# Preparing the state stage's weights on GpSimd instead of VectorE, at the start of the attention stage

## What is computed

```python
x = x + _L0_conv_ref(_gn(x), ...)   # 7x7 window attention, 4 heads of 8
x = x + _L1_conv_ref(_gn(x), ...)   # depthwise convolution, state-space scan, gated output
x = x + _L2_conv_ref(_gn(x), ...)   # triangular products over rows, layer norm, gate
x = x + _L3_conv_ref(_gn(x), ...)   # LSTM over the 28 rows
```

```python
def _L1_conv_ref(x, w1, dw, in_proj_w, conv1d_w, ..., x_proj_w, dt_proj_w, ..., out_proj_w, ..., w2, wout):
    x1 = _grouped_1x1(x, w1)                       # 4 groups of 8 channels
    x1 = depthwise_conv_3x3(x1, dw); x1 = silu(x1)
    x1 = _mamba(x1.reshape(B, H * W, D), ...)      # in_proj, 3-tap conv1d, x_proj, dt_proj, scan, out_proj
    x1 = layer_norm(x1) * gamma + beta
    return _grouped_1x1(x1 * silu(_grouped_1x1(x, w2)), wout)
```

## Time and profile before

| | |
|---|---|
| median of 3 runs | 478.54 us (476.59 to 478.87) |
| the profiled execution | 475.85 us, span 474.1 us |
| TensorE busy | 351.1 us, 74% |
| VectorE busy | 365.1 us, 77% |
| ScalarE busy | 299.8 us, 63% |
| GpSimd busy | 233.9 us, 49% |
| mean granted TensorE clock | 0.901 of full |
| attention stage | about 21 to 158 us |

### The profile page before, as it was taken

One profiled execution on the slowest core, in us unless ns is written; L12 is line 12 of the kernel. 1 busy time (PEld: TensorE's weight loads), 2 busy tenths in 40 slices (PEclk: granted clock), 3 DMA queues, 4 the chain that ended last, 5 costly groups with the idle time before them and its releaser, 6 DMA issues. The chain is left out here.

```text
span 474.1 us, 10021 instructions
## 1 busy us (share of the span) xinstructions
PE 351.1 (74%) x3480; PEld 230.4 (49%) x3480; DVE 365.1 (77%) x679; ACT 299.8 (63%) x583; POOL 233.9 (49%) x217
## 2 busy tenths in 40 slices
PE   5149888896789785985877647666795829888885
PEld 4037676675665332142233213222483519877774
DVE  3799999999797388799787999997576685544443
ACT  4327788887785899578758946347985253333432
POOL 4526868775673324966972999567081130000000
PEclk9997999998899999599897885768999668999999
DMA  6110000000223231022000000000030000111111
GB/s 147 5 18 3 3 1 0 0 1 0 59 60 70 51 87 29 1 60 58 1 0 1 0 1 0 0 0 1 3 68 3 1 0 11 20 19 22 22 19 24
DMA packets 24044, 10.29 MB, mean 22 GB/s; under 512 B 20576, under 2 KB 22368, under 8 KB 24016
## 3 DMA queue, kind: packets, MB, share of 16 engines
q1 hardware_dynamic: 23888, 9.93, 10.3%
q0 software_dynamic: 128, 0.01, 0.2%
HBM read 2.00 MB, written 1.61 MB: 8 GB/s over the span
## 5 line engine op out<-in xcount | busy, mean ns | idle before, releaser
L480 POOL TENSOR_TENSOR Pr<-Pr,rc 128x392 f32<-128x392 f32 x64 | 54.4, 883 | 32.2 <-DVE rc L1826 32.2
L511 POOL TENSOR_TENSOR YA<-YA,hC 128x784 f32<-128x784 f32 x27 | 51.7, 1914 | 32.4 <-DVE hC L1910 31.5
L1349 PE MATMUL pair<-BCf,sel 96*128 96x392 bf16 x128 | 38.4, 394 | 35.0 <-DVE Hs L1894 30.8
L1894 DVE TENSOR_TENSOR_SCAN Hs<-dA,pair 128x784 f32<-128x784 f32 x32 | 57.1, 1785 | 1.0
L1193 PE MATMUL pair<-ident,Pr 128*128 128x128 f32 x256 | 41.1, 293 | 13.2 <-ACT PT L715 9.0
L1349 PEld LDWEIGHTS pair<-BCf,sel 96*128 96x128 bf16 x128 | 10.2, 105 | 74.0 <-issue 71.6
L1193 PEld LDWEIGHTS pair<-ident,Pr 128*128 128x128 f32 x256 | 29.2, 146 | 25.1 <-ACT PT L715 15.8
L1887 DVE TENSOR_TENSOR pair<-DU,pair 128x784 f32<-128x784 f32 x32 | 31.1, 973 | 10.6 <-PE pair L1349 10.3
L715 ACT ACTIVATE PT<-pair 128x392 f32<-128x392 f32 x64 | 31.4, 497 | 5.9 <-PE pair L1193 5.6
L724 ACT ACTIVATE Pr<-Ts 128x392 f32<-128x392 f32 x64 | 32.5, 536 | 3.4 <-DVE Ts L1810 3.4
L1804 DVE TENSOR_REDUCE mx<-pair 128x8 f32<-128x392 f32 x64 | 32.6, 550 | 1.6 <-PE pair L1150 1.4
(11 more groups left out here) (262 smaller groups left out, 928.8 us busy)
## 6 DMA issues: line engine op xcount, KB each, us to landing
SX<-XP SPq DMA_DIRECT2D x48, 112.2 KB
XT<-in_x SPq DMA_DIRECT2D x4, 392.0 KB, 5.0
out<-Os SPq DMA_DIRECT2D x28, 56.0 KB, 1.8
AD<-Aa SPq DMA_DIRECT2D x4, 196.0 KB
NB<-in_L_conv_x_proj_w SPq DMA_DIRECT2D x4, 3.0 KB
DW<-in_L_conv_dw SPq DMA_DIRECT2D x4, 1.1 KB
vec<-in_L_conv_b_qkv POOLq DMA_DIRECT2D x3, 0.5 KB, 5.8
W<-in_L_conv_w_qkv SPq DMA_DIRECT2D x1, 48.0 KB
```

What stands on the lines that cost most here:

```text
L480: eng.tensor_tensor(pg, pg, bcast(rc[:, g, :], 2, WT), ALU.mult).then_inc(pn_r, 1)
L511: eng.tensor_tensor(y, y, hC[:, n % NHC, :], ALU.add).then_inc(g_ya, 1)
L1349: ins = eng.matmul(SPREAD[s][:, columns(h)], sel[:, n, :], upper(BCf[:, c % 2, s, columns(h)]), start=True, stop=True)
L1894: eng.tensor_tensor_scan(Hs[:, n % 2, :], dA[:, n % NA, :], SPREAD[0], 0.0, ALU.mult, ALU.add).then_inc(v_s, 1)
```

## The change

GpSimd does the 15 products ahead of round -1, once VectorE has made mask8 and the DMAs have landed. VectorE waits for them, transposes, and keeps the mean steps, U_DL and the bias. GpSimd copies into W4 and W3 (now straight from TB) behind round 0, spreads BD behind round 1, and makes WBC behind round 2, ahead of clearing XP. maskz goes. VectorE's links ahead of the transpose fall from 4 to 1, so TRB is 2. s_hf counts GpSimd's steps up to 8, s_sel has two more increments on VectorE, and TensorE waits for s_hf = 8 ahead of the first convolution and for s_sel = 3 ahead of the scan.

```diff
-        maskz = sb("maskz", [P, G])
...
-        TRB = 5
+        TRB = 2
...
             for m in (xw, Qw, Vst, Pr):
                 eng.memset(m[:], 0.0).then_inc(s_mk2, 1)
             eng.wait_ge(s_mk2, 1)
+            eng.wait_ge(s_sel, 1)
+            loaded(eng, 1)
+            for k, dst in ((0, W8X[:, :]), (1, NB[:, 1, :]), (2, NB[:, 2, :])):
+                ins = eng.tensor_tensor(dst.rearrange("p (h i) -> p h i", h=4), bcast(W8[:, k, :], 1, 4), bcast(mask8[:, :], 2, 8), ALU.mult)
+            ins.then_inc(s_hf, 1)
+            for k in range(3):
+                eng.tensor_scalar(NB[:, 4 + k, :], WIN[:, 0, :], C1[:, k:k + 1], None, ALU.mult)
+            eng.wait_ge(s_hf, 2)
+            for k in range(9):
+                ins = eng.tensor_scalar(NB[:, 7 + k, :], W8X[:, :], DW[:, k:k + 1], None, ALU.mult)
+            ins.then_inc(s_hf, 1)
...
-            for s in (-1, 0, 1, 2):
-                pool_att(s, s % 2)
+            pool_att(-1, 1)
+            pool_att(0, 0)
+            eng.wait_ge(s_sel, 2)
+            eng.tensor_copy(W4[:, U_Z:U_DL, :], TB[:, 0:U_DL - U_Z, :]).then_inc(s_hf, 1)
+            for x in range(3):
+                rows = slice(C * x, C * x + C)
+                eng.wait_ge(s_hf, 4 + x)
+                eng.tensor_copy(W3[rows], TB[rows, U_DL - U_Z + x:16:3, :]).then_inc(s_hf, 1)
+            eng.wait_ge(s_hf, 7)
+            pool_att(1, 1)
+            eng.tensor_tensor(BD[:, U_Z:U_CV, :].rearrange("p u (g c) -> p u g c", g=G), bcast(W4[:, U_Z:U_CV, :], 2, G),
+                              bcast(bcast(bd[:, :], 1, U_CV - U_Z), 3, C), ALU.mult)
+            pool_att(2, 0)
+            for s in range(2):
+                for q in range(3):
+                    ins = eng.tensor_tensor(WBC[:, s, C * q:C * q + C].rearrange("p (g n) -> p g n", g=G),
+                                            bcast(TB[:, 17, R + DS * s:R + DS * s + DS], 1, G), bcast(bd[:, :], 2, DS), ALU.mult)
+            ins.then_inc(s_hf, 1)
             eng.memset(XP[:, :, :], 0.0).then_inc(s_bd, 1)
...
             pe_att(15, 1)
-
+            eng.wait_ge(s_hf, 8)
...
             conv(1, 1)
-            eng.wait_ge(s_sel, 1)
+            eng.wait_ge(s_sel, 3)
...
-            eng.tensor_reduce(mask8[:, :], m16[:, :].rearrange("p (g h) -> p h g", g=G), AX.X, ALU.add)
+            eng.tensor_reduce(mask8[:, :], m16[:, :].rearrange("p (g h) -> p h g", g=G), AX.X, ALU.add).then_inc(s_sel, 1)
...
-            loaded(eng, 1)
-            link(eng.tensor_tensor(maskz[:, :], m8[:, 0:4], m8[:, 4:8], ALU.add))
-
-            for k, dst in ((0, W8X[:, :]), (1, NB[:, 1, :]), (2, NB[:, 2, :])):
-                ins = eng.tensor_tensor(dst.rearrange("p (h i) -> p h i", h=4), bcast(W8[:, k, :], 1, 4), bcast(mask8[:, :], 2, 8), ALU.mult)
-            link(ins)
-            for k in range(3):
-                eng.tensor_scalar(NB[:, 4 + k, :], WIN[:, 0, :], C1[:, k:k + 1], None, ALU.mult)
-            for k in range(9):
-                ins = eng.tensor_scalar(NB[:, 7 + k, :], W8X[:, :], DW[:, k:k + 1], None, ALU.mult)
-            link(ins)
+            eng.wait_ge(s_hf, 3)
             link(eng.transpose(TB[:, :, :].rearrange("p u c -> p (u c)"), NB[:, :, :].rearrange("p u c -> p (u c)")))
...
-            eng.tensor_copy(W4[:, U_Z:U_DL, :], TB[:, 0:U_DL - U_Z, :])
-            link(eng.tensor_copy(W4[:, U_CV:NU, :], TB[:, U_DL - U_Z:16, :]))
-            for x in range(3):
-                rows = slice(C * x, C * x + C)
-                eng.tensor_copy(W3[rows], W4[rows, U_CV + x:NU:3, :])
             eng.wait_ge(s_wd, 1)
             eng.tensor_copy(W4[:, U_DL, :], banks[7][:, 0:C])
-            link(eng.tensor_tensor(vec[:, V_BZF:V_BZF + 1], vec[:, V_BZ:V_BZ + 1], banks[7][:, C:C + 1], ALU.add))
-            spread_weights(U_Z, U_CV)
-            for s in range(2):
-                for q in range(3):
-                    eng.tensor_tensor(WBC[:, s, C * q:C * q + C].rearrange("p (g n) -> p g n", g=G),
-                                      bcast(TB[:, 17, R + DS * s:R + DS * s + DS], 1, G), bcast(bd[:, :], 2, DS), ALU.mult)
+            eng.tensor_tensor(vec[:, V_BZF:V_BZF + 1], vec[:, V_BZ:V_BZ + 1], banks[7][:, C:C + 1], ALU.add).then_inc(s_sel, 1)
```

## The result

The changed kernel took 481.34 us (median of 5 runs, 479.58 to 481.91), the kernel before 476.59 in the five runs beside it (470.71 to 478.87). The ratio is 1.0147, with a 95% interval of 1.0075 to 1.022: slower. Two more sets gave 1.0128 [1.0065, 1.0192] and 1.0106 [1.0057, 1.0155]. The absolute forecast of 480.9 hit, but against 478.54; the kernel before has a median of 476.3 to 476.8 over the 23 to 35 runs of a set. These ratios leave out executions more than 1.5% above the fastest of their kernel; over all executions the medians are 4.75, 2.87 and 3.77 us apart, 0.6 to 1.0%.

What follows compares the result with a forecast made beforehand. VectorE was taken to set the pace of the attention loop. Terms 0.55 + 1.85 + 1.56 - 1.57 = +2.4 us on 478.54 gave 480.9 us, own range 479.9 to 482.7, with rivals 477.9 to 483.2.

Steps and rivals of the forecast that it cites:

- L1759's stall: VectorE's weight preparation before strip 0: one product held up behind GpSimd's Km, about 1.26 us, gone with the change.
- the idle time of 1.57 us behind Km: GpSimd's queue from Km's end at 49.22 to Pr's products at 50.80: spare time that the inserted work uses up, -1.57 us.
- Rival (a): GpSimd's queue in the attention loop: the inserted work is hidden and VectorE keeps its 0.84 us lead, 477.7 us; chance 0.12.
- (c): Start of attention: the transpose is held behind GpSimd's xw and Km until 29.4, total +4.2 us, 482.7; chance 0.07.
- part 3: VectorE losing preparation work: strip 0 leads by 0.84 us, but from the exp wait at 43.39 it is 0.55 us late.
- part 6: Six WBC products on GpSimd behind strip 2, ahead of clearing XP: 1.56 us, bounds 1.4 and 2.4.
- GpSimd's part: Lateness through GpSimd's queue up to Km ahead of strip 4: 0.55 + 1.85 + 1.56 - 1.57 = +2.4 us.
- The lead of 0.84 us in strip 0: VectorE, freed of work, starts strip 0 at about 31.0, 0.84 us earlier than before; the lead does not last.
- the last part of the sum: V waits for xw, scores for Km, so VectorE's strip 4 begins at about 60.95 instead of 58.57.
- the clock as a rival only: TensorE's low clock at 36 to 42 us: absent, 478.7, chance 0.08; lasting another strip, 482.9, chance 0.08.
- the lateness is carried to the end: From strip 4 on VectorE is busy almost without a gap, so the +2.4 us stays and nothing is caught up.
- The base: Whole kernel before the change: the median of 478.54 us to which the forecast added 2.4 us.

Runs made afterwards that it cites:

- e2: The changed kernel with its 15 products put back on VectorE; copies, spread and WBC stay on GpSimd: ratio 1.0077 to the kernel before.
- e3: The changed kernel with GpSimd's clearing of XP behind round 4 instead of round 2: ratio 1.0050 to the kernel before.
- e7: e2's kernel with GpSimd's spread in halves behind rounds 1 and 2, WBC in halves behind 3 and 4, XP's clearing behind 6: ratio 0.9995.
- e10: The kernel before, with GpSimd also clearing an unread tile (about 3.1 us) behind XP, behind round 2: ratio 1.0065 to the kernel before.
- e4: The kernel before again, no edit, for a second profile: ratio 1.0019 to itself.
- e0: The changed kernel again, no edit, second profile: ratio 1.0128 to the kernel before; the profiled execution took 474.87 us.
- e8: The changed kernel a third time, no edit: ratio 1.0106 to the kernel before.
- e1: The kernel before with only the 15 products moved to GpSimd, everything behind the transpose left on VectorE: ratio 1.0034 to the kernel before.

## Why the prediction was wrong

**Right: the mechanism and its place.** The transpose was at 27.88 (forecast 27.57, range 27.2 to 28), L1759's stall is gone, the spread took 1.89 us (1.9), the idle time of 1.57 us behind Km was used up (0.25 left), V of strip 4 waited 1.50 us for xw where 2.5 was forecast (V of strip 3 0.44 where 1.5 was), and strip 4 was at 61.30 where 60.95 was forecast, behind a wait of 2.56 instead of 1.5. e2, e3, e7 and e10 show that GpSimd's queue makes the wait. Rival (a), hidden work, fell by e2; (c), a colliding transpose, by its 0.78 us beside xw. The estimate of 2.45 us for the spread from the Trainium skill (GPSIMD Engine Reference, Engine selection: about twice as slow) was too high: the row says 1.89, 1.54 times VectorE's 1.23.

**The terms of the sum that were off.** In part 3, "0.55 late" from the exp of strip 1: VectorE did not wait there at all, and Pr of strip 1 began at 43.83 instead of 44.74, as the scores of strip 1 took 0.95 us instead of 2.58: a short stretch of full clock fell on them. In part 6, WBC took 1.23 us instead of 1.56 and held the queue for 1.16. With 0.25 us of idle time left over, these made GpSimd's part +1.35 instead of +2.4 (2.4 - 0.9 - 0.4 + 0.25). The lead of 0.84 us in strip 0, which rival (a) rests on, did not exist either: from the start of the scores to the first max it takes 1.73 us there (30.20 to 31.93), where I had put 1.05. The row was there: in the kernel before, strip 0's scores took 1.64 us at 29.22, the length at half clock, while the clock column says 1.00 for that stretch. TensorE was at half clock there already, and the column does not show it.

**The step that failed** is in the last part of the sum: "V waits for xw, the scores for Km, and VectorE's strip 4 begins at about 60.95", with V, attention product and scores at their old lengths, which are those of full clock. I had the clock as a rival only, and at the stretch from 36 to 42 us. It fell at 58 instead, behind the very wait that the change makes: 0.68 us between V and scores and 0.71 in the scores, 1.4 of the 2.73 us at strip 4, which the sum has at nothing. Wrong sizes of both signs cancelled, so strip 4 agreed by luck. In two of three profiles of the changed kernel that stretch was at half clock, in none of the two of before. For the total it was another step that failed: "the lateness is carried to the end", with nothing added behind 146 us. In the first profile 2.94 us at softplus became 5.90 at the triangular stage, with the clock at 0.78 instead of 0.84 in the stretch named under e4; in e0, against e4, 3.1 us became 1.4. What places those low stretches stays open.

**What was missed in the total.** From XN's start strip 4 is 42.0 us away in the changed kernel (mean of three) and 39.3 before (two): 2.7 us, 0.57%. The three ratios are 1.0106 to 1.0147, or 5 to 7 us; the medians differ by 3 to 5. Part of the gap is scatter, and part may be the state stage: its mean over the three profiles is 1.4 us longer than over the two of before (180.8 against 179.4), which with the 2.7 would make 4.1. It has three lengths, and the longest stood in two of three profiles of the changed kernel and in three of ten of the others. That is too few to tell. e0 shows that the change alone does not bring it; whether it makes it more frequent stays open. The base was wrong too: 478.54 was the median of three runs, and later sets give 476.3 to 476.8.

## What to carry to other kernels

An engine that is busy half of the time can still have no room: read its slack where the work goes in, strip by strip, and put in pieces that are smaller than it. 1.9 and 2.8 us at once cost 1.7 us at strip 4 here (e2), 1.4 of it in half clock behind the wait, and the same work in pieces of at most 1.6, at most one to a strip and XP's clearing put later, cost nothing measurable (e7). Work that is needed late is better put into the same engine's own long wait (3.47 us in round 12, filled from round 11) than on another engine; and a wait for it should not stand in an in-order queue ahead of the work that starts a stage. Where a change makes TensorE wait, put the products behind the wait at half clock as one end of the range, and read the clock from the lengths of like products too, as the column can miss a stretch.

## What was not expected of the hardware

Products behind waits of 1.50, 1.51 and 3.89 us ran at half clock: scores 1.64 us instead of 0.95, the attention product 1.54 instead of 0.91. Behind a wait of 1.22 us they didn't (e8). The clock column and the lengths disagree in the first 40 us: strip 0's scores took 1.64 us in all three profiles of the changed kernel and in both of before, with the column at 1.00; in e1 the same 1.64 stands beside 0.50. GpSimd's two-input products of 32 columns follow each other every 0.2 us, its products with a per-partition scalar every 0.33 (3.01 us for nine, 352 ns each). The state stage of one and the same kernel took 177.5 us in one execution and 182.6 in another.
